# A quarter of the attention's softmax sums moved from ScalarE passes to GpSimd additions, with a shorter fill between indirect transfers and a new order

## The chip, the cores and the metric

The kernel runs on one core of one Trainium2 chip. The metric is the device time in microseconds of one execution. TensorE (PE) does the matmuls, with its weight loads listed as PEld; VectorE (DVE) and ScalarE (ACT) work on PSUM and SBUF; GpSimd (POOL) works on SBUF and issues the indirect transfers; SyncE (SP) issues the other transfers.

## What is computed

Input x has 16 batches of 512 tokens with 128 features. Three sublayers follow each other, each on the layer norm of x and added to x:

```python
x = x + 0.5 * ffn(layernorm(x))      # stage A
x = x + attention(layernorm(x))      # stage B
x = x + 0.5 * ffn(layernorm(x))      # stage C

def ffn(x):                          # 8 experts of 256 hidden units, the best 2 of each token
    probs = softmax(x @ gate_w.T + gate_b)
    vals, idx = top_k(probs, 2)
    y = relu(x @ w1[e] + b1[e]) @ w2[e] + b2[e]     # for the two experts
    return sum(y * vals)

def attention(x):                    # 8 heads of 32, 512 x 512 scores per head and batch
    q = x @ Wq.T
    k, v = (x @ Wkv_down.T) @ Wk_up.T, (x @ Wkv_down.T) @ Wv_up.T
    attn = softmax(q @ k.T * 32 ** -0.5)
    return (attn @ v) @ Wo.T
```

All data are float32.

## The kernel before

**Stages and steps.** The work is cut into named steps, keyed by stage, batch (or chunk of batches), name and number. Stages A and C route their tokens in chunks of 1 to 3 batches: gate logits, the two best experts (top1, top2, gate), the ranks of the tokens within each expert (rank1, rank2), a scatter of token rows to slots in DRAM (scat, two indirect transfers per 128 tokens on POOL), loads of four slot tiles at a time and of their experts' weights (xload, wload on SP), the expert's two products (xg, h, y), a store of the results (ystore), a gather of each token's two results (gat, two indirect transfers on POOL) and their weighted addition to x (comb, DVE). The first batch in A and the last in C are done densely instead, over all eight experts (dh, dy).

**Attention.** Each batch has two groups of four heads, and each group four tiles of 128 rows. The steps of a group are, in order:

- max or rmax: PE makes the scores with queries as rows, 4 matmuls of 128x512 per step into 4 PSUM banks; DVE takes each row's negated maximum (line 1538, neg_m). In rmax ACT then makes a second pass over the same bank (line 1199): exp(score - maximum) in place, with the row sum accumulated into `sums`; the bank is free after that. In max the bank is free after DVE.
- msplit or rsplit: rsplit takes the logarithm of the sums on ACT (line 1206) and subtracts it from neg_m on DVE (line 1545); both then split neg_m into a high and a low part. mrow: PE turns these into rows.
- s: PE makes the transposed scores and adds the rows from mrow; ACT takes the exponential into `probs` (line 1190), 4 passes of 128x512 per step, 4 steps. `probs` holds one group.
- pv: PE multiplies `probs` with V, 16 matmuls; ACT copies the result to `o_n` (line 1211).
- For a group that isn't by rows: add (line 1056), POOL adds probability tiles in pairs into `pairs`, four 128x512 additions after the second s step and four after the fourth; sum (lines 1268, 1560 and 1822): PE multiplies `pairs` with ones, 8 matmuls; ACT takes 1/sum as exp(-ln); DVE refines that and multiplies `o_n` by it. For a group by rows the probabilities are normalized already and neither step exists.
- wo: after both groups, PE multiplies `o_n` with Wo, and DVE adds it to x.

`by_rows(b, g)` at line 62 says which way a group goes; before the change it is true for all 32 groups, and no add or sum step is made. The lines that ACT's first s step waits for are at 1186: with a group before it that isn't by rows, it waits for that group's last addition (p_added). `previous_added` finds the last such group, whose `pairs` must have been read.

**The order.** A planner in the kernel's file (`all_steps`, `plan`) lays out every engine's instructions once, when the program is built. Each step has a due time, worked out from the constants at lines 90 to 100, and a cost per engine in the table PARTS (line 176; an addition on POOL stands at 1.27 us). Whenever an engine is free, the planner gives it the ready step with the earliest due time. On the chip each engine runs its list strictly in that order and waits on semaphores. Rings limit what is under way: 8 PSUM banks in all, and up to 8 for rmax, 7 for steps that DVE reads, 6 for steps that ACT reads.

**The fill.** POOL's steps scat and gat issue two indirect transfers each. Between two such steps that follow each other directly, POOL first writes the tile `pause` (line 1072, a memset of 128x900) and waits for it. The planner keeps such steps GAP (3.4 us) apart.

Of the kernel before, what the change touches and what calls it, by code (L numbers as in the profile page):

```python
# [12 lines left out]
P = 128  # L13
# [30 lines left out]
def n_quads(c):  # L44
    return (n_tiles(c) + 3) // 4
# [14 lines left out]


def by_rows(b, g):
    return True


def previous(b, g):
# [3 lines left out]
def previous_added(b, g):  # L70

    b, g = previous(b, g)
    while b >= 0 and by_rows(b, g):
        b, g = previous(b, g)
    return b, g


def max_name(b, g):
    return "rmax" if by_rows(b, g) else "max"


def split_name(b, g):
    return "rsplit" if by_rows(b, g) else "msplit"
# [3 lines left out]

PERIOD, FIRST_B = 54.81, 448.4  # L90
WANTED = {"norm": -306.42, "scaled": 175.09, "xT": -0.86, ("q", 0): -510.52, ("k", 0): -55.28, ("v", 0): 51.75,
          ("v", 1): 77.62, ("q", 1): -259.95, ("k", 1): -286.69, "wo": -16.36}
GROUP_GAP, MAX_PACE, S_FIRST, S_PACE, PV, ADD, SUM = -6.56, 9.75, -155.58, 14.86, -20.5, 31.84, 190.16
A_LEAD, A_PACE, A_ROUTE, A_NORMS = 1.91, 10.45, 102.08, 3.43
C_NORM, C_ROUTE, C_FIRST, C_PACE, C_GATHER = 70.53, 4.33, 52.37, 59.65, -48.02
LOAD_AHEAD, W_AHEAD = -185.66, -51.27
B_SHIFT = [-90.73, 208.24, -383.83, -10.9, 27.39, -56.91, -109.2, -98.67, -258.75, 51.94, -111.41, -70, -88.21, -77.68, 72.17, 64.26]
A_SHIFT = [-175.05, -104.61, -123.83, -99.41, 64.11, 103.6, 44.98]
C_SHIFT = [47.89, 123.22, 85.45, 65.66, 50.22, -503.25, 389.89]
GAP = 3.4  # L100


def wanted_attention(b):

    at = {}
    for name in ("norm", "scaled", "xT"):
        at[name, 0] = WANTED[name]
    at["wo", 0] = WANTED["wo"]
    for name, k in (("q", 0), ("k", 0), ("v", 0), ("v", 1), ("q", 1), ("k", 1)):
        at[name, k] = WANTED[name, k]  # L110
    for g in range(GROUPS):
# [8 lines left out]
        if not by_rows(b, g):  # L120
            at["sum", g] = at["pv", g] + SUM
    return {("B", b, name, k): FIRST_B + PERIOD * b + B_SHIFT[b] + t for (name, k), t in at.items()}


def wanted_experts(s, c):
# [3 lines left out]
    dense = c == DENSE[s]  # L129
    shift = (A_SHIFT if s == "A" else C_SHIFT)[c - CHUNKS_OF[s][0]]  # L130
    quads = 0 if dense else n_quads(c)
# [308 lines left out]
def plan(steps):  # L440
# [21 lines left out]
    def note(t, kind, step, part):  # L462
        nonlocal counter
        counter += 1
        put(events, (t, counter, kind, step, part))
# [5 lines left out]
    def may_begin(step):  # L471
        nonlocal next_comb
        if step.part == 0:
# [12 lines left out]
            if step.name == "comb" and combs[next_comb] != step.key[:2]:  # L486
                return False
            if step.name in ("scat", "gat") and now < indirect + GAP:
                return False
# [8 lines left out]
    while True:  # L498
        progress = True
        while progress:  # L500
            progress = False
            for e in ENGINES:
# [10 lines left out]
                if step.part == 0:  # L513
# [21 lines left out]
                    if step.name in ("scat", "gat"):  # L535
                        indirect = now
                        note(now + GAP, "look", step, 0)
                length = step.parts[step.part][1]
# [162 lines left out]
def macaron_kernel(nc, x, wq, wkv_down, wk_up, wv_up, wo, gate_w, gate_b, w1, b1, w2, b2, out):  # L701
# [41 lines left out]
    with ExitStack() as ctx:  # L743
        def sb(name, shape, dt=F32):
            return ctx.enter_context(nc.sbuf_tensor(name, shape, dt))
# [8 lines left out]
        gw_T, gate_bias = sb("gw_T", [P, EXPERTS]), sb("gate_bias", [P, EXPERTS])  # L754
        first_wins = sb("first_wins", [P, EXPERTS])
        ident = sb("ident", [P, P])
        pause = sb("pause", [P, 900])
        ones = sb("ones", [P, P])
        minus_one = sb("minus_one", [1, P])
        earlier = sb("earlier", [P, P])  # L760
# [1118 lines left out]
```

## Time and profile before

| | |
|---|---|
| median of 3 runs | 1188.9 us (1188.76 to 1192.47) |
| the profiled execution | 1187.95 us |
| its span, first to last instruction | 1186.2 us |
| mean granted TensorE clock | 0.978 of full |
| matmul records, weight-load records | 8142, 8142 |

The page of a profile gives each engine's busy time in the span, the chain of work that ended last (followed back from the last instruction, at each step to what released it), and the costliest groups of instructions. Other views answer for a stretch of time: busy time of each engine, the chain by line, or the instructions in order of time. A float32 matmul leaves two records. Matmuls are pipelined and their ends are modelled, so a busy PE isn't a PE at its peak. All matmuls outside transposes have the helper's line, 1584, so they are told apart by the tiles that they read. A row of busy time by stretch gives the stretch, its length, then PE, PEld, DVE, ACT and POOL with their instructions.

### The profile page before, as it was taken

What the parts mean: (1) busy time and instruction counts of PE and PEld (TensorE: products, weight loads), DVE (VectorE), ACT (ScalarE), POOL (GpSimd) and SP (SyncE); (2) the same over time, 40 slices, a digit from 0 to 9 for tenths busy, and PEclk for the clock granted to TensorE, in tenths of its full rate; (3) what the DMA queues carried; (4) which work ended last, traced back from release to release, by engine and by line L of the source; (5) the groups of instructions that cost most, each with busy time, mean ns of one, the idle gap of its engine ahead of it and who ended that gap; (6) DMA issues with size and microseconds to landing.
All of it is one profiled execution on the core that took longest, in us unless ns stands there. A gap on an engine that the chain in (4) does not pass through costs nothing.

```text
span 1186.2 us, 25770 instructions
## 1 busy us (share of the span) xinstructions
PE 1116.0 (94%) x8142; PEld 736.6 (62%) x8142; DVE 720.2 (61%) x2254; ACT 910.1 (77%) x2255; POOL 712.1 (60%) x868
## 2 busy tenths in 40 slices
PE   5989998999999999999999999999999999999896
PEld 3657575676675557566665666666665446657574
DVE  4766468576785557376664686556556646557335
ACT  2339678788897989797898888888888988788431
POOL 3136558674758888028888643886602885268555
PEclk9979998999999999999999999999999999999988
DMA  8074573856645177656565636576732155648872
GB/s 288 2 273 146 176 210 111 257 155 207 205 136 152 45 224 218 174 154 201 173 199 167 180 113 193 154 221 183 210 107 65 39 181 158 184 142 242 256 239 74
DMA packets 159882, 202.05 MB, mean 170 GB/s; under 512 B 16938, under 2 KB 103426, under 8 KB 159747
## 3 DMA queue, kind: packets, MB, share of 16 engines
q1 hardware_dynamic: 144196, 168.90, 46.5%
q0 software_dynamic: 15360, 31.49, 9.1%
q8 instruction: 67, 1.10, 0.4%
q14 instruction: 67, 0.55, 0.2%
q10 hardware_dynamic: 192, 0.02, 0.0%
HBM read 152.50 MB, written 47.84 MB: 169 GB/s over the span
## 4 chain that ended last, share of the span: by engine, by line
PE 70%; ACT 17%; DVE 4%; POOL 4%; issue 3%; DMA 2%; SPq 0%; POOLq 0%; ACTq 0%; DVEq 0%
PE psum L1584 65%; ACT psum L1199 7%; ACT probs L1190 6%; PE psum L1702 2%; POOL Y L1108 2%; DVE neg_m L1538 2%; PE psum L1767 1%; ACT hg L1236 1%; POOL pause L1072 1%; PE psum L1669 1%; ACT xnB L1155 1%; DMA results_C<-ys 1%; DMA xs<-slots_C 1%; DVE neg_hl L1557 0%; PE psum L1662 0%
## 5 line engine op out<-in xcount | busy, mean ns | idle before, releaser
L1538 DVE TENSOR_REDUCE neg_m<-psum 128x1 f32<-128x512 f32 x512 | 317.4, 682 | 153.1 <-PE psum L1584 152.9
L1584 PE MATMUL psum<-nat 32*128 32x512 f32 x2048 | 362.4, 637 | 0.9 <-ACT nat L1266 0.4
L1199 ACT ACTIVATE psum<-psum,neg_m 128x512 f32<-128x512 f32 x512 | 341.0, 680 | 26.5 <-DVE neg_m L1538 25.8
L1190 ACT ACTIVATE probs<-psum 128x512 f32<-128x512 f32 x512 | 266.4, 631 | 42.7 <-PE psum L1584 42.4
L1584 PEld LDWEIGHTS psum<-nat 32*128 32x128 f32 x2048 | 130.5, 184 | 93.4 <-issue 25.5
L1584 PEld LDWEIGHTS psum<-xg_T,wt 128*128 128x128 f32 x1296 | 157.4, 195 | 43.7 <-ACT probs L1190 13.6
L1072 POOL MEMSET pause<- 128x900 f32 x212 | 183.3, 865 | 0.1
L1584 PE MATMUL psum<-xg_T,wt 128*128 128x128 f32 x1296 | 172.5, 283 | 7.9 <-DMA wt<-packed 6.0
L1088 POOL DMA_INDIRECT slots_A<-xnA,posA x120 | 117.6, 980 | 91.0 <-DMA xs<-slots_A 40.9
L1584 PEld LDWEIGHTS psum<-wt,hg 128*128 128x128 f32 x1296 | 151.9, 192 | 31.6 <-ACT psum L1199 11.8
L1108 POOL DMA_INDIRECT Y<-results_C,posC x120 | 115.6, 963 | 90.2 <-issue 69.7
L1584 PE MATMUL psum<-wt,hg 128*128 128x128 f32 x1296 | 162.2, 278 | 7.9 <-ACT hg L1236 3.7
L1088 POOL DMA_INDIRECT slots_C<-xnC,posC x120 | 117.0, 975 | 56.5 <-DVE posC L1487 21.2
L1108 POOL DMA_INDIRECT Y<-results_A,posA x120 | 115.6, 963 | 57.4 <-issue 30.3
L1584 PE MATMUL psum<-m_rows,heads_one 32*128 32x512 f32 x512 | 126.9, 751 | 0.0
L1236 ACT ACTIVATE hg<-psum 128x512 f32<-128x512 f32 (+1 forms) x168 | 96.8, 621 | 35.2 <-PE psum L1584 35.1
L1584 PE MATMUL psum<-probs,V 128*32 128x512 f32 x1024 | 117.6, 600 | 5.5 <-ACT probs L1190 5.2
L1518 DVE TENSOR_TENSOR ys<-psum,wt 128x512 f32<-128x512 f32 x84 | 56.7, 675 | 99.3 <-PE psum L1584 98.9
L1199 ACT ACTIVATION_READ_ACCUMULATOR psum<-psum,neg_m 128x1 f32 x512 | 115.8, 226 | 0.0
L1123 POOL TENSOR_SCALAR xnC<-X,rstdC,shiftC 128x128 f32<-128x128 f32 x64 | 28.5, 454 | 119.1 <-DVE shiftC L1370 118.8
L1584 PEld LDWEIGHTS psum<-probs,V 128*32 128x32 f32 x1024 | 31.6, 110 | 73.3 <-issue 59.8
L1211 ACT ACTIVATE o_n<-psum 128x512 f32<-128x512 f32 x32 | 19.1, 596 | 54.1 <-PE psum L1584 53.8
(190 smaller groups left out, 1382.2 us busy)
## 6 DMA issues: line engine op xcount, KB each, us to landing
wt<-packed SPq DMA_DIRECT2D x324, 320.0 KB
xs<-slots_A SPq DMA_DIRECT2D x36, 256.0 KB
results_A<-ys SPq DMA_DIRECT2D x36, 256.0 KB
xs<-slots_C SPq DMA_DIRECT2D x36, 256.0 KB
results_C<-ys SPq DMA_DIRECT2D x36, 256.0 KB
X<-in_L_attn_x_dram SPq DMA_DIRECT2D x16, 256.0 KB, 7.9
out_dram<-X SPq DMA_DIRECT2D x16, 256.0 KB
packed<-probs SPq DMA_DIRECT2D x1, 2560.0 KB, 8.2
```

What stands on the lines that cost most here:

```text
L1072: linked(pool.memset(pause[:], 0.0))
L1088: pool.indirect_dma_start(out=slots[s][:], out_offset=bass.IndirectOffsetOnAxis(ap=pos[s, c % C_RING][:, k, t:t + 1], axis=0), in_=xn[s][: ...
L1108: pool.indirect_dma_start(out=Y[:, i % Y_RING, k, n, :], out_offset=None, in_=results[s, c][:], in_offset=bass.IndirectOffsetOnAxis(ap=pos ...
L1123: last = pool.tensor_scalar(xn[s][:, xn_place(s, b) + n, :], X[:, b % X_RING, n, :], rstd[s][:, n:n + 1], shift[s][:, n:n + 1], ALU.mult, ...
L1190: act.activation(probs[:, kt, j, :], at.banks()[j][:], ACT.Exp).then_inc(a_done, 1)
L1199: act.activation(at.banks()[j][:], at.banks()[j][:], ACT.Exp, bias=neg_m[:, g, n, j:j + 1], accum_out=sums[:, g, n, j:j + 1]).then_inc(S[" ...
L1211: act.activation(o_n[:, at.k, :], bank[:], ACT.Copy).then_inc(a_done, 1)
L1236: act.activation(hg[:, i % HG_RING, 0:n, :, :].rearrange("p n u t -> p (n u t)"), bank[:, 0:n * UNITS * P], ACT.Relu).then_inc(a_done, 1)
L1518: V_.tensor_tensor(ys[:, i % YS_RING, 0:len(tiles), :], bank[:, 0:len(tiles) * P].rearrange("p (i d) -> p i d", d=D), wt[:, first:first + ...
L1538: V_.tensor_reduce(neg_m[:, g, n, j:j + 1], at.banks()[j][:], AX.X, ALU.max, negate=True).then_inc(S["r_done"], 1)
L1584: return nc.tensor.matmul(dst, w, m, start=start, stop=stop)
L1702: last = nc.tensor.transpose(bank[:, tokens(n)], xs[:, i % XS_RING, n, :], ident[:])
```

## The change

`by_rows` becomes true for group 1 of every batch and group 0 of the even batches: group 0 of the 8 odd batches, a quarter of the groups, now takes max, msplit, add and sum instead of rmax and rsplit. The tile `pause` shrinks from 900 to 400 columns, and the planner's GAP from 3.4 to 2.95 us. All due-time constants are new, so the order of every engine is laid out anew. Costs in PARTS, rings and buffers stay.

```diff
 def by_rows(b, g):
-    return True
+    return g == 1 or b % 2 == 0
...
-PERIOD, FIRST_B = 54.81, 448.4
-WANTED = {"norm": -306.42, "scaled": 175.09, "xT": -0.86, ("q", 0): -510.52, ("k", 0): -55.28, ("v", 0): 51.75,
-          ("v", 1): 77.62, ("q", 1): -259.95, ("k", 1): -286.69, "wo": -16.36}
-GROUP_GAP, MAX_PACE, S_FIRST, S_PACE, PV, ADD, SUM = -6.56, 9.75, -155.58, 14.86, -20.5, 31.84, 190.16
+PERIOD, FIRST_B = 55.55, 516.37
+WANTED = {"norm": -221.79, "scaled": 160.9, "xT": 66.34, ("q", 0): -644.14, ("k", 0): -62.88, ("v", 0): 53.33,
+          ("v", 1): 27.43, ("q", 1): -402.5, ("k", 1): -375.9, "wo": 48.96}
+GROUP_GAP, MAX_PACE, S_FIRST, S_PACE, PV, ADD, SUM = -42.62, 6.88, -135.18, 13.63, -2.2, 24.62, 228.05
...
-GAP = 3.4
+GAP = 2.95
...
-        pause = sb("pause", [P, 900])
+        pause = sb("pause", [P, 400])
```

The lines left out between SUM and GAP are the other due-time constants (A_LEAD to C_SHIFT), all with new values.

## Rows read from the trace of the kernel before

**Rows 1.** The page's head: busy us, share of the span, instructions of each engine.

```profile
span 1186.2 us, 25770 instructions
...
PE 1116.0 (94%) x8142; PEld 736.6 (62%) x8142; DVE 720.2 (61%) x2254; ACT 910.1 (77%) x2255; POOL 712.1 (60%) x868
```

**Rows 2.** The chain that ended last: by engine (page), by line (whole chain).

```profile
PE 70%; ACT 17%; DVE 4%; POOL 4%; issue 3%; DMA 2%; SPq 0%; POOLq 0%; ACTq 0%; DVEq 0%
...
by line: PE psum L1584 64.9%; ACT psum L1199 6.8%; ACT probs L1190 6.4%; issue 3.3%; PE psum L1702 2.3%; POOL Y L1108 1.8%; DVE neg_m L1538 1.5%; PE psum L1767 1.2%; ACT hg L1236 0.9%; POOL pause L1072 0.8%; PE psum L1669 0.8%; ACT xnB L115
```

**Rows 3.** Busy us by stretch and engine; clock, DMA share, GB/s.

```profile
918.00:962.00 44.00, 41.04 (x233) 20.83 (x229) 25.16 (x55) 41.48 (x107) 36.40 (x42) 1.00 0.17 52
200.00:1100.00 900.00, 874.09 (x6598) 562.98 (x6590) 558.11 (x1645) 764.90 (x1907) 564.23 (x646) 1.00 0.56 168
```

**Rows 4.** Chain by line: 200 to 1100, 918 to 962, 420 to 441.

```profile
by line: PE psum L1584 71.1%; ACT psum L1199 8.4%; ACT probs L1190 7.2%; PE psum L1702 2.6%; issue 1.9%; PE psum L1767 1.5%; ACT xnB L1155 0.9%; ACT hg L1236 0.8%; DVE neg_m L1538 0.8%; DMA xs<-slots_C 0.7%; PE psum L1669 0.7%; PE psum L166
...
by line: ACT psum L1199 41.8%; ACT probs L1190 31.3%; PE psum L1584 13.4%; DVE neg_hl L1557 3.0%; issue 2.3%; DVE neg_m L1538 1.6%; PE psum L1767 1.5%; ACT m_rows L1215 1.4%; ACT nat L1266 1.1%; ACT V L1175 1.1%; ACT log_sums L1206 0.7%; AC
...
by line: PE psum L1584 64.4%; DMA xs<-slots_C 30.3%; PE psum L1702 6.2%; issue 0.6%
```

**Rows 5.** Instruction groups: count, busy us, mean ns, idle us before and releasers.

```profile
L1199 ACT ACTIVATE psum<-psum,neg_m 128x512 f32<-128x512 f32 x512 | 341.0, 680 | 26.5 <-DVE neg_m L1538 25.8
...
L1190 ACT ACTIVATE probs<-psum 128x512 f32<-128x512 f32 x512 | 266.4, 631 | 42.7 <-PE psum L1584 42.4
...
L1523 DVE TENSOR_TENSOR X<-psum,X 128x512 f32<-128x512 f32 x16 | 10.9, 684 | 8.9 <-PE psum L1584 8.9
...
L1206 ACT ACTIVATE log_sums<-sums 128x16 f32<-128x16 f32 x32 | 8.0, 250 | 0.4
```

**Rows 6.** Timeline 920 to 938 us: start, us, engine, line, idle before.

```profile
922.59 0.66 ACT L1199 ACTIVATE psum<-psum,neg_m 128x512 f32<-128x512 f32 x1
...
923.26 0.65 ACT L1199 ACTIVATE psum<-psum,neg_m 128x512 f32<-128x512 f32 x1
...
924.59 0.66 ACT L1199 ACTIVATE psum<-psum,neg_m 128x512 f32<-128x512 f32 x1
...
924.75 0.29 PEld L1584 LDWEIGHTS psum<-nat 32*128 32x128 f32 x2 [0.38 <-ACT psum L1199]
```

**Rows 7.** Timeline from 470 us: batch 5, last s pass, pv, next group.

```profile
473.65 2.08 ACT L1190 ACTIVATE probs<-psum 128x512 f32<-128x512 f32 x4
...
475.82 3.64 PE L1584 MATMUL psum<-probs,V 128*32 128x512 f32 x32 [0.26 <-ACT probs L1190]
...
479.39 1.14 PE L1584 MATMUL psum<-nat 32*128 32x512 f32 x8
...
480.79 2.06 ACT L1190 ACTIVATE probs<-psum 128x512 f32<-128x512 f32 x4 [0.67 <-PE psum L1584]
```

**Rows 8.** POOL's instruction groups, columns as in rows 5.

```profile
L1072 POOL MEMSET pause<- 128x900 f32 x212 | 183.3, 865 | 0.1
...
L1123 POOL TENSOR_SCALAR xnA<-X,rstdA,shiftA 128x128 f32<-128x128 f32 x64 | 27.7, 442 | 48.6 <-DVE shiftA L1370 46.6 <-DMA slots_A<-xnA,posA 1.7
...
L1034 POOL MEMSET ones<- 128x128 f32 x1 | 0.2, 201 | 0.0
```

**Rows 9.** The end: chain by line from 1108 us, timeline from 1170.

```profile
by line: POOL Y L1108 26.8%; issue 17.9%; POOL pause L1072 12.1%; DMA results_C<-ys 11.8%; PE psum L1584 7.1%; ACT probs L1190 3.7%; DMA Y<-results_C,posC 3.1%; DVE X L1503 2.6%; SPq L996 2.2%; SPq L997 2.1%; POOLq L743 1.5%; DVE X L1462 1.
...
1172.03 3.73 PE L1584 MATMUL psum<-probs 128*128 128x128 f32 x32
...
1174.17 0.86 POOL L1072 MEMSET pause<- 128x900 f32 x1
...
1176.57 0.95 POOL L1108 DMA_INDIRECT Y<-results_C,posC  x1 [0.30 <-issue]
1179.04 2.31 DVE L1503 SCALAR_TENSOR_TENSOR X<-Y,gateC,X 128x128 f32<-128x128 f32 x8 [3.17 <-DMA Y<-results_C,posC]
...
1181.99 1.13 DVE L1462 SCALAR_TENSOR_TENSOR X<-psum,givenC,X 128x128 f32<-128x128 f32 x4
```

More of the change, by code:

```diff
@@ L83, in split_name @@
     return "rsplit" if by_rows(b, g) else "msplit"
-PERIOD, FIRST_B = 54.81, 448.4
-WANTED = {"norm": -306.42, "scaled": 175.09, "xT": -0.86, ("q", 0): -510.52, ("k", 0): -55.28, ("v", 0): 51.75,
-          ("v", 1): 77.62, ("q", 1): -259.95, ("k", 1): -286.69, "wo": -16.36}
-GROUP_GAP, MAX_PACE, S_FIRST, S_PACE, PV, ADD, SUM = -6.56, 9.75, -155.58, 14.86, -20.5, 31.84, 190.16
[L94 to L99, printed above, removed]
-GAP = 3.4
+PERIOD, FIRST_B = 55.55, 516.37
+WANTED = {"norm": -221.79, "scaled": 160.9, "xT": 66.34, ("q", 0): -644.14, ("k", 0): -62.88, ("v", 0): 53.33,
+          ("v", 1): 27.43, ("q", 1): -402.5, ("k", 1): -375.9, "wo": 48.96}
+GROUP_GAP, MAX_PACE, S_FIRST, S_PACE, PV, ADD, SUM = -42.62, 6.88, -135.18, 13.63, -2.2, 24.62, 228.05
+A_LEAD, A_PACE, A_ROUTE, A_NORMS = 20.81, 7.22, 126.74, 5.62
+C_NORM, C_ROUTE, C_FIRST, C_PACE, C_GATHER = 45.48, 46.92, 69.4, 56.84, -148.48
+LOAD_AHEAD, W_AHEAD = -228.24, -52.47
+B_SHIFT = [-112.91, 194.63, -374.71, -81.81, 45.44, -91.1, -114.34, -112.13, -293.69, 43.01, -104.38, 4.57, -63.69, -89.57, 34.33, 66.2]
+A_SHIFT = [-283.55, -71.81, -31.91, -95.18, 13.23, 110.89, 85.61]
+C_SHIFT = [22.45, 143.53, 208.16, 83.05, -88.11, -661.1, 395.16]
+GAP = 2.95
 def wanted_attention(b):
```

## The prediction

> **What bounds the kernel now.** I read the page's head first: TensorE (PE) is busy for 94% of the span, ScalarE (ACT) for 77%, VectorE (DVE) 61% and GpSimd (POOL) 60% [rows 1]. A PE that is busy for 94% looks like the bound, so the second view is the chain of work that ended last, and it says something more careful: 70% of the span hangs on PE, but 17% on ACT, and of that 6.8% of the span (0.068 x 1186.2 = 81 us) on line 1199 and 6.4% (76 us) on line 1190 [rows 2]. Line 1199 is the second pass over the score rows that makes the softmax sums (step rmax); line 1190 makes the probabilities (step s).
>
> The third view is busy time by stretch. From 200 to 1100 us, PE is busy for 874 of 900 us and ACT for 765. From 918 to 962 us PE still shows 41.0 of 44 us, yet ACT is at 41.5 there [rows 3], and the chain of that stretch is ACT: 41.8% on line 1199 and 31.3% on line 1190, against 13.4% on PE's line 1584 [rows 4]. So a busy PE in that stretch is a PE that crawls: its matmuls are spread out by the wait for a free PSUM bank. The timeline shows it: ACT starts a pass every 0.67 us (922.59, 923.26, ..., 924.59) and PE's weight loads wait 0.38 us on line 1199 for the bank that such a pass gives back [rows 6]. In other stretches the same step costs nothing: from 420 to 441 us, where batch 5's group 0 makes its maxima and sums, line 1199 isn't on the chain at all [rows 4]. The kernel is thus bound by PE for most of the time and by ACT in patches of the attention.
>
> The end is a third regime. After the last attention step the chain runs through POOL's gathers, and 12.1% of the last 79 us, 9.6 us, is the fill (pause) between them, that is 11 of them [rows 9].
>
> **The change part by part.**
>
> **ACT is relieved.** Group 0 of each odd batch, 8 of 32 groups, goes from rmax/rsplit to max/msplit. That takes 8 x 16 = 128 passes of line 1199 away, at a spacing of 0.67 us: -86 us of ACT time [rows 5, 6], and 8 logarithms of 0.25 us: -2 us [rows 5]. Each sum step gives ACT a logarithm and an exponential of 128x512 back, at about 0.63 us as line 1190's: 8 x 2 x 0.63 = +10 us [rows 5]. Net -78 us of 910. Only what is on the chain counts. A quarter of line 1199's 81 us is -20 us. From one side this could be 0, if the chain's patches lie in the other groups, as between 420 and 441 us. From the other it could be about -39 us, if the s passes that queue behind the removed ones leave the chain in the same proportion ((81 + 76) / 4). I take -20: it is the mean over all groups. The 10 us of added ACT work count by ACT's 17% of the chain: +2 us.
>
> **PE gets eight sum steps.** Each is 8 matmuls of ones with 32 output rows, four of which share a round as those of pv do: pv's 16 take 479.39 - 475.82 = 3.57 us [rows 7], so 8 take 1.79 us and the eight steps 14.3 us. Nothing on PE goes away: the maxima's matmuls stay. At PE's 70% of the chain this is +10 us; the ends are 0, if all of it falls into ACT's patches, and +14.3 us.
>
> **DVE.** Its maxima stay. The three operations per sum step, near 0.68 us each as line 1523's [rows 5], add 8 x 3 x 0.68 = 16 us to an engine at 61%, while group 1 is still being worked; wo needs them only after group 1's pv. Nothing on the path, 0. If the cover failed (wo waiting for the sum), the whole step would show, 1.8 on PE, 2 x 0.63 on ACT and 3 x 0.68 on DVE, about 5 us in each odd batch. Where msplit replaces rsplit the wait for ACT's logarithm falls out, on the path perhaps -1 us.
>
> **POOL gets 64 additions of 128x512**, which the trace doesn't show. From below: a memset of 128 columns takes 0.20 us and one of 900 takes 0.865 us, 0.86 ns a column, so 512 columns that are only written take 0.53 us. From above: a tensor_scalar of 128 columns takes 0.44 us and four of them 1.77 us [rows 8], or 3.5 us if a second input costs as much again. An addition reads SBUF as the tensor_scalar does, in one instruction instead of four, so I take a value near its first figure, 1.4 us; the kernel's own cost table counts 1.27. 64 x 1.4 = 90 us, and the shorter fill gives 212 x 0.43 = 92 us back (below), so POOL's load stays. The Trainium skill speaks against this move: "GPSIMD Engine Reference", section 4.1 Engine selection, sends additions of a tile to VectorE, since a two-input operation is about twice as slow on GpSimd. No row here shows such an operation on GpSimd; with line 1523's 684 ns the rule would make an addition an estimated 1.4 us and leave the sum as it is. At the tensor_scalar's 3.5 us the sum would be 12 us higher (below).
>
> **A new wait.** ACT's first probability pass of the next group waits for the last addition, because the additions read the single buffer of probabilities. Queued behind it on ACT are all later passes, and PE waits for the banks they empty. Four additions come after a group's last s pass: 4 x 1.4 = 5.6 us. Today the next group's first pass starts 480.79 - 475.73 = 5.1 us after the end of that last pass (473.65 + 2.08), behind pv [rows 7]. The additions are then 0.5 us late by themselves; POOL works in order, and half a spacing of the indirect transfers under way (1.5 us) comes on top: about 2 us in each of 8 groups, 16 us of ACT time, of which 17% reaches the end: +3 us. Ends: 0 at 0.53 us an addition; at 3.5 us they are 9 + 1.5 us late, 84 us of ACT time and +14 us, some 12 above what I take; and +16 us if PE has no expert work to put into the 2 us.
>
> **The fill.** By the two memset rows 400 columns take 0.20 + 272 x 0.00086 = 0.43 us instead of 0.865: -0.43 us a pause. At the end 11 of them are on the chain: -4.8 us. There PE finishes its last matmuls at 1175.8 us and POOL issues its last gather at 1176.57; the combination on DVE starts at 1179.04 and the last expert's additions, which stood behind it, end at 1183.1 [rows 9]. PE's end is just behind POOL's, so the dense expert is late next: of the 4.8 us I count -4; ends 0 and -5. At the start, the first scatter and gather have about three pauses each, -2 us if they are on the path; I count -1.
>
> **The replanned order.** The due times change everywhere. The trace gives no price for that; I count 0. From the stretch of 200 to 1100 us, where 26 of 900 us are idle on PE [rows 3], an order better or worse by about half of that is plausible: -12 to +12 us.
>
> **The sum:** -20 + 2 + 10 - 1 + 3 - 4 - 1 = -11 us. The profiled execution took 1187.95 us with a span of 1186.2; the median of the runs is 1188.9, 0.95 us above it. 1187.95 - 11 = 1177, and about 1178 for a median.
>
> **The rivals.**
>
> *PE pays in full (slower).* Place: PE's stretches where its line 1584 makes up the chain, 71.1% from 200 to 1100 us [rows 4]. If ACT's patches lie in groups that keep their row sums, the relief is near 0, while the sums cost 14.3 us, the late additions 3 and the fill gives 5 back: 1189 + 12 = 1201 us. It decides once less than 8 us of the relief reaches the chain. For it: the stretch at 420 us. Against it: that of 920 us, in which batch 13's group 0 has its passes, with line 1199 on 41.8% of the chain [rows 4].
>
> *Late additions (slower).* If additions stand behind two spacings of indirect transfers (2 x 2.95 us, the plan's new gap) and cost 1.77 us each, ACT restarts 13 us after the last pass instead of 5: up to 8 x 8 = 64 us of ACT time; a third of it at the end gives about 1189 - 11 + 21 = 1199 us, more if PE runs dry. Against it: POOL is idle for 40% of the span [rows 1].
>
> *The whole patch goes (faster).* Relief of -39 instead of -20: 1159 us, with a better order down to 1150.
>
> *No difference.* Relief and sums cancel, and only the fill is left, or an order that is worse by some 8 us: 1186 to 1192 us.
>
> *The fill isn't what spaces the transfers*, so shortening it does nothing: the pauses on the chain, each between two gathers [rows 9], speak against it; it would cost the 5 us of gain, 1183 us.
>
> **How the numbers follow.** Forecast (1164 to 1185, the fill's rival in it): 0.45. Whole patch: 0.11. No difference, within 0.3% (3.6 us, about what a measurement of this kernel can tell): 0.14. PE in full: 0.20. Late additions: 0.10. So faster 0.56, same 0.14, slower 0.30. The forecast's own range is 1164 to 1185. The range for 8 in 10 takes in most of both slower rivals and of the whole patch: 1152 to 1206.
>
> **What would show it.** Right: line 1199 with 384 passes and about 85 us less busy; ACT's share of the chain near 15.5% (202 - 18 of 1175 us), PE's near 71.5% (830 + 10); 128 records of ones with pairs, two per matmul, eight matmuls spaced 1.8 us in all; pauses of 0.43 us and a tail shorter by 4 us; additions of 1.2 to 1.6 us, with ACT's wait on them under 2 us. Wrong: ACT's share of the chain still at 17% with PE's work 14 us longer; waits of line 1190 on POOL's additions of 5 us and more; a later end of the dense expert in the tail; idle PE in the middle beyond today's 26 us, which would put the loss on the new order.

## The result, and the profile after

The changed kernel takes 1208.8 us (median of four runs, 1203.9 to 1215.0) against 1189.2 us (median of four): 1.0146 times the time before, with a 95% interval of 1.0115 to 1.0176. The ratios here and below are those on record, from runs side by side; they aren't the quotients of the medians (here 1.016). A second measurement of the same code gave 1207.9 us and 1.0151 [1.0096, 1.0206]. The forecast was 1178 us in a range of 1152 to 1206; the sign is wrong and the time lies outside the range.

The profiled execution took 1215.0 us with a span of 1212.9, and is the slowest of the four. From its page come the span, the busy times, the granted TensorE clock in 40 slices, and the groups of the moved step (busy us, mean ns, idle us before and what ended it):

```profile
span 1212.9 us, 25879 instructions
...
PE 1142.3 (94%) x8270; PEld 748.9 (62%) x8270; DVE 747.0 (62%) x2270; ACT 837.6 (69%) x2007; POOL 697.8 (58%) x917
...
PEclk9978998999999898999889999999999989999989
...
L1199 ACT ACTIVATE psum<-psum,neg_m 128x512 f32<-128x512 f32 x384 | 255.8, 680 | 25.0 <-DVE neg_m L1538 24.2
...
L1064 POOL TENSOR_TENSOR pairs<-probs 128x512 f32<-128x512 f32 x64 | 79.9, 1280 | 34.6 <-ACT probs L1190 34.5
L1072 POOL MEMSET pause<- 128x400 f32 x197 | 88.5, 449 | 0.1
...
L1827 PE MATMUL psum<-pairs,ones 128*32 128x512 f32 x128 | 15.4, 598 | 0.7 <-ACT psum L1199 0.7
```

Nearly all of what the change says has happened. Line 1199 has 384 passes instead of 512 and is busy for 85.2 us less [rows 5], an addition takes 1.28 us, a pause 0.45 us, the eight sum steps 15.4 us on PE, and ACT is down from 910.1 to 837.6 us, by 72.5 [rows 1]. Two lines don't fit a kernel that lost work. DVE rose by 26.8 us [rows 1], where 16 us of sums were expected. And the clock row, nothing but nines from the eighth slice to the 38th before, has five slices with an 8 there, while PE stays at 94% busy.

The stretch from 200 to 1100 us shows why the busy share misled (stretch, length, then PE, PEld, DVE, ACT and POOL with their instructions, granted clock, DMA share, GB/s):

```profile
200.00:1100.00 900.00, 879.09 (x6554) 565.25 (x6554) 570.14 (x1632) 696.04 (x1684) 528.48 (x655) 0.97 0.54 161
```

PE is idle for 20.9 us here, less than the 25.9 us before [rows 3]. But it left 6554 matmul records instead of 6598, although the whole kernel has 128 more, and its granted clock is 0.97 instead of 1.00. Against the kernel before, the time didn't go into idle PE; PE runs slower here. The order differs, though, and with it the work that falls into the stretch. The kernel new_writes (below) has the changed kernel's own order, and against it both show, 7.2 us more of idle PE and a lower clock. Its row:

```profile
200.00:1100.00 900.00, 886.27 (x6739) 569.86 (x6740) 562.91 (x1671) 707.90 (x1717) 530.29 (x671) 0.99 0.55 166
```

To find the places I compared when each batch's output addition starts (line 1523, the sixteen times in order) with the same times of a kernel that differs only in what POOL does in place of the additions (new_writes, below). The changed kernel falls behind in jumps: +3.4 us in batch 1, +5.4 in batch 5, +7.1 in batch 7, +4.4 in batch 13 and +3.3 in batch 15, and by no more than 0.5 us in any other batch. All are odd batches, the ones with additions. These two profiles stand at opposite ends, the slowest of four runs against the fastest of ten (1190.5 us), so the jumps add up to more than the 15 us between the kernels' runs. A second profile of the changed kernel (changed_again, 1207.9 us, at its median) starts 2.2 us ahead of new_writes and is 17.1 us behind at batch 15, with +3.8 us in batch 1, +3.9 in batch 5, +1.7 in batch 7, +2.6 in batch 9, +4.2 in batch 13 and +3.3 in batch 15: odd batches again.

Batch 5's jump, in order of time (start, us, engine, line, idle before and what ended it):

```profile
466.50 0.16 DVE L1361 SCALAR_TENSOR_TENSOR ntC<-ntC,vepsC 128x4 f32<-128x4 f32 x1
...
467.58 4.94 POOL L1064 TENSOR_TENSOR pairs<-probs 128x512 f32<-128x512 f32 x4 [2.05 <-ACT probs L1190]
...
467.85 1.01 DVE L1360 TENSOR_TENSOR ntB<-rstdB 128x4 f32<-128x4 f32 x1 [0.60 <-ACT rstdB L1147]
...
468.90 1.20 DVE L1361 SCALAR_TENSOR_TENSOR ntB<-ntB,vepsB 128x4 f32<-128x4 f32 x1
...
470.13 1.19 DVE L1362 SCALAR_TENSOR_TENSOR rstdB<-ntB,rstdB 128x4 f32<-128x4 f32 x1
...
471.35 1.19 DVE L1369 TENSOR_TENSOR shiftB<-mvB,rstdB 128x4 f32<-128x4 f32 x1
...
472.65 2.48 DVE L1538 TENSOR_REDUCE neg_m<-psum 128x1 f32<-128x512 f32 x4
...
472.78 1.65 ACT L1155 ACTIVATE xnB<-X,shiftB,rstdB 128x128 f32<-128x128 f32 x4 [3.50 <-DVE shiftB L1370]
...
475.14 1.36 PE L1584 MATMUL psum<-nat 32*128 32x512 f32 x3 [2.80 <-ACT psum L1199]
```

Four additions run on POOL from 467.58 to 472.52. Beside them DVE works through four operations on 128x4 elements, the normalisation's Newton step and shift. Each has two inputs in SBUF and takes 0.16 us where POOL adds nothing (so at 466.50, a microsecond earlier); here each takes as long as an addition. The chain is done at 472.7 instead of some 469. ACT waits 3.50 us for it, the maxima on DVE (line 1538) stand behind it, and PE runs dry for 2.80 us.

The other jumps have the same form. Between 195 and 1125 us PE is idle for more than 1.3 us at a time in five places: 1.81 us before 239 us (batch 1), 2.80 before 475 (batch 5), 1.36 before 599 (batch 7), 2.35 before 981 (batch 13) and 1.66 before 1113 (batch 15). In the ten us ahead of each, DVE instructions are held beside additions. In new_writes no idle time of PE in that stretch is longer than 1.14 us. Batch 13's is the plainest, with the low part of the negated maxima (line 1558) held and PE waiting for it:

```profile
977.50 4.95 POOL L1064 TENSOR_TENSOR pairs<-probs 128x512 f32<-128x512 f32 x4 [6.46 <-ACT probs L1190]
...
980.07 1.20 DVE L1558 TENSOR_TENSOR neg_hl<-neg_m,neg_hl 128x16 f32<-128x16 f32 x1
...
981.41 0.76 PE L1767 MATMUL psum<-ident,neg_hl 128*128 128x128 f32 x4 [2.35 <-DVE neg_hl L1558]
```

After a stall the clock can follow. Three stretches of ten us around batch 5's, columns as above, for the changed kernel:

```profile
455.00:465.00 10.00, 9.57 (x74) 6.43 (x71) 9.29 (x33) 9.97 (x27) 7.97 (x11) 1.00 0.60 183
465.00:475.00 10.00, 7.34 (x60) 5.11 (x52) 9.05 (x22) 6.47 (x18) 7.46 (x8) 1.00 0.64 181
475.00:485.00 10.00, 9.86 (x46) 6.08 (x47) 5.05 (x24) 8.47 (x23) 4.66 (x7) 0.66 0.76 227
```

In the last one PE is busy for 9.86 us with only 46 matmuls, at a mean granted clock of 0.66: by the trace's clock records it stood at the lower level, 1.2 GHz, from 476.6 to 483.4 us. So the stall of some 3 us is paid a second time in slow matmuls. The two profiles of the changed kernel give a price for that. In changed_again the same stall (2.81 us) is followed by 3.4 us at the lower level instead of 6.8, and the jump is 3.9 us instead of 5.4; in batch 7 the same stall (1.35 us) is followed by none instead of 13.7 us in two patches, and the jump is 1.7 us instead of 7.1. By these two pairs a microsecond at the lower level cost about 0.4 us (an estimate: 1.5 us over 3.4, and 5.4 over 13.7). Over the whole span the records show 94.6 us at the lower level in 12 patches; before it was 52.4 us in 7.

Counted over the trace, 26 DVE instructions beside an addition last over 0.15 us longer than the median of their group, together 31.7 us: lines 1360, 1361, 1362 and 1369 of the normalisation, 1441, 1443, 1476, 1478 and 1484 of the routing, 1545, 1557 and 1558 of msplit and rsplit, and 1503. Before, a different pair did this: 41 DVE instructions beside a pause of 900 columns, 27.3 us in all.

The Trainium skill has this rule on its page "SBUF — State Buffer", section "Who interferes with whom": a DVE instruction with two SBUF inputs contends with a GpSimd instruction that reads SBUF, though not with one that only writes it, and copies, casts and tensor_scalars in their two-port mode contend with any; the loser waits for the whole instruction. The trace agrees in kind, with 1.01 to 1.20 us beside additions of 1.28 us on average. It is the rule that spoke against this change, and the prediction didn't weigh it.

### The profile page after: what moved, and what is told of

It reads as the page before. It is cut to its first block and busy times, and to the rows that moved or that the text cites. A ratio compares the mean times of both kernels' runs of the same rounds, so it can differ in the third digit from the quotient of the medians.

```text
span 1212.9 us, 25879 instructions
## 1 busy us (share of the span) xinstructions
PE 1142.3 (94%) x8270; PEld 748.9 (62%) x8270; DVE 747.0 (62%) x2270; ACT 837.6 (69%) x2007; POOL 697.8 (58%) x917
## 5 line engine op out<-in xcount | busy, mean ns | idle before, releaser
L1199 ACT ACTIVATE psum<-psum,neg_m 128x512 f32<-128x512 f32 x384 | 255.8, 680 | 25.0 <-DVE neg_m L1538 24.2
L1584 PEld LDWEIGHTS psum<-xg_T,wt 128*128 128x128 f32 x1296 | 165.2, 201 | 46.6 <-ACT probs L1190 14.8
L1584 PE MATMUL psum<-xg_T,wt 128*128 128x128 f32 x1296 | 182.0, 290 | 3.5 <-DMA wt<-packed 3.0
L1108 POOL DMA_INDIRECT Y<-results_A,posA x120 | 115.3, 961 | 72.5 <-issue 37.1
L1584 PE MATMUL psum<-m_rows,heads_one 32*128 32x512 f32 x512 | 130.3, 787 | 0.0
L1518 DVE TENSOR_TENSOR ys<-psum,wt 128x512 f32<-128x512 f32 x84 | 56.0, 668 | 72.3 <-PE psum L1584 63.6
L1064 POOL TENSOR_TENSOR pairs<-probs 128x512 f32<-128x512 f32 x64 | 79.9, 1280 | 34.6 <-ACT probs L1190 34.5
L1072 POOL MEMSET pause<- 128x400 f32 x197 | 88.5, 449 | 0.1
L1199 ACT ACTIVATION_READ_ACCUMULATOR psum<-psum,neg_m 128x1 f32 x384 | 86.5, 225 | 0.0
```

What stands on the lines that cost most here:

```text
L1064: pool.tensor_tensor(pairs[:, kt // 2, j, :], probs[:, kt - 1, j, :], probs[:, kt, j, :], ALU.add).then_inc(S["p_added"], 1)
L1072: linked(pool.memset(pause[:], 0.0))
L1108: pool.indirect_dma_start(out=Y[:, i % Y_RING, k, n, :], out_offset=None, in_=results[s, c][:], in_offset=bass.IndirectOffsetOnAxis(ap=pos ...
L1199: act.activation(at.banks()[j][:], at.banks()[j][:], ACT.Exp, bias=neg_m[:, g, n, j:j + 1], accum_out=sums[:, g, n, j:j + 1]).then_inc(S[" ...
L1518: V_.tensor_tensor(ys[:, i % YS_RING, 0:len(tiles), :], bank[:, 0:len(tiles) * P].rearrange("p (i d) -> p i d", d=D), wt[:, first:first + ...
L1584: return nc.tensor.matmul(dst, w, m, start=start, stop=stop)
```

## The experiments

Those that rest on the kernel before are named old_..., those on the changed kernel new_.... An inserted line moves the line numbers behind it by one to three.

**The cause: what the additions do to others.** new_writes puts a memset of 1020 columns in each addition's place and lets it wait for the one before, so POOL is busy nearly as long but reads nothing; the ones' product reads a constant.

```diff
-                pool.tensor_tensor(pairs[:, kt // 2, j, :], probs[:, kt - 1, j, :], probs[:, kt, j, :],
-                                   ALU.add).then_inc(S["p_added"], 1)
+                if (at.index, at.k) == (1, GROUP):
+                    pool.memset(pairs[:], 1.0)
+                wait(pool, S["p_added"], counts["p_added", at.step] - 1)
+                pool.memset(written[:], 0.0).then_inc(S["p_added"], 1)
```

> The changed kernel, order unchanged; each addition is replaced by a memset of 1020 columns and a wait for the one before it, about the time of an addition, which reads no SBUF (the sums are then constants). In the changed kernel's trace 26 VectorE instructions, most with two SBUF inputs, are stretched by 31.7 us in all beside additions. If that blocking is what stalls TensorE and lowers its clock: 1193 to 1203 us, with these instructions at their usual length. If only the additions' time and place count: 1206 to 1212 us.

It took 1194.7 us, 1.0019 [0.9998, 1.0041] times the time before: by the two ratios 1.3% less than the changed kernel, 15 us. The same place in its timeline, and the same stretches:

```profile
464.00 4.15 POOL L1068 MEMSET written<- 128x1020 f32 x4 [1.74 <-ACT probs L1193]
...
464.30 0.16 DVE L1363 TENSOR_TENSOR ntB<-rstdB 128x4 f32<-128x4 f32 x1 [0.61 <-ACT rstdB L1150]
...
464.89 0.16 DVE L1372 TENSOR_TENSOR shiftB<-mvB,rstdB 128x4 f32<-128x4 f32 x1
465.09 0.95 DVE L1373 TENSOR_SCALAR shiftB<-shiftB 128x4 f32<-128x4 f32 x1
...
466.07 1.65 ACT L1158 ACTIVATE xnB<-X,shiftB,rstdB 128x128 f32<-128x128 f32 x4 [0.35 <-DVE shiftB L1373]
...
465.00:475.00 10.00, 9.91 (x70) 6.49 (x67) 7.83 (x29) 9.62 (x26) 8.45 (x11) 1.00 0.94 276
475.00:485.00 10.00, 10.00 (x87) 5.30 (x89) 1.40 (x3) 5.34 (x12) 7.87 (x9) 1.00 0.46 138
```

Beside writes the four operations take 0.16 us again; the tensor_scalar behind them (line 1373 here) is the one that is held up, for 0.95 us. ACT waits 0.35 us instead of 3.50, PE doesn't stall, and the clock stays at 1.00. DVE's busy time falls from 747.0 to 720.7 us and the time at the lower clock from 94.6 to 52.7 us. The memsets aren't free for DVE either: 17 instructions are held beside them, by 14.3 us in all, but PE doesn't stall for it. The memset's series is shorter than the additions' (4.15 against 4.94 us), so a little of the 15 us could be POOL's time; the next kernel bounds that.

new_addtiny replaces each addition by a memset of a single column: no reads, and hardly any time on POOL.

```diff
-                pool.tensor_tensor(pairs[:, kt // 2, j, :], probs[:, kt - 1, j, :], probs[:, kt, j, :],
-                                   ALU.add).then_inc(S["p_added"], 1)
+                if (at.index, at.k) == (1, GROUP):
+                    pool.memset(pairs[:], 1.0)
+                n = counts["p_added", at.step] - 1
+                pool.memset(ticks[:, n:n + 1], 0.0).then_inc(S["p_added"], 1)
```

> The changed kernel, order unchanged; each addition is replaced by a memset of one column, about 0.1 us (the sums are then constants): POOL's 80 us, the blocking of VectorE and nearly all of ScalarE's wait for the last addition are gone, the sum steps stay. If additions cost the changed kernel its loss: 1185 to 1197 us. If the loss lies in the order and in TensorE's sums: 1203 to 1209 us.

1192.4 us, 0.9991 [0.9972, 1.0009]: only 0.28%, 3.3 us, below new_writes, with intervals that overlap, though POOL is busy for another 58.2 us less. POOL's time and the holding that memsets do are worth some 3 us; what hurts is the reading. Its time at the lower clock is 68.4 us, more than new_writes' 52.7, and it is still no slower: the microseconds at the lower level aren't a measure of the loss by themselves.

**Shorter blocks?** If a blocked operation waits for one POOL instruction, four pieces of 128 columns would cut the wait to a quarter. changed_again is the changed kernel itself beside it.

```diff
-                pool.tensor_tensor(pairs[:, kt // 2, j, :], probs[:, kt - 1, j, :], probs[:, kt, j, :],
-                                   ALU.add).then_inc(S["p_added"], 1)
+                for n in range(4):
+                    part = slice(n * P, (n + 1) * P)
+                    last = pool.tensor_tensor(pairs[:, kt // 2, j, part], probs[:, kt - 1, j, part], probs[:, kt, j, part], ALU.add)
+                last.then_inc(S["p_added"], 1)
```

> The changed kernel, order unchanged; each addition of 512 columns is made in four instructions of 128. POOL's time for them goes up by its fixed part, some 0.1 us an instruction, 20 us in all. Theory blocking for the length of one GpSimd instruction: each stretched VectorE instruction loses about 0.4 us instead of up to 1.2, so some 20 of 32 us go; ratio 1.002 to 1.010 in spite of longer additions. If VectorE has to wait until GpSimd has no reading instruction left, or if the additions' length counts instead: 1.014 to 1.025.

> The changed kernel as it is, beside the others of this set on the same chip. If its loss holds against the kernel before: ratio 1.010 to 1.018, with TensorE at half clock for 80 to 105 us and VectorE instructions stretched by about 30 us beside additions.

new_chop4 took 1216.7 us, 1.0215 [1.0187, 1.0242], the changed kernel beside it 1207.9, 1.0151 [1.0096, 1.0206]: no better. Its group of additions, then a stretch of its timeline:

```profile
L1066 POOL TENSOR_TENSOR pairs<-probs 128x128 f32<-128x128 f32 x256 | 109.2, 463 | 18.7 <-ACT probs L1192 18.5
...
860.78 6.63 POOL L1066 TENSOR_TENSOR pairs<-probs 128x128 f32<-128x128 f32 x16
...
862.53 4.50 DVE L1547 TENSOR_TENSOR neg_m<-neg_m,log_sums 128x16 f32<-128x16 f32 x1 [2.08 <-ACT log_sums L1208]
...
867.82 0.45 PE L1769 MATMUL psum<-ident,neg_hl 128*128 128x128 f32 x1 [3.15 <-DVE neg_hl L1560]
```

Four pieces cost 1.85 us instead of 1.28. In many places the hold did shrink with the pieces: three of batch 5's four operations take 0.38 or 0.39 us each instead of 1.19 or 1.20, and batches 5 and 7 fall behind new_writes by 2.1 and 1.2 us. But one operation of 128x16 elements, 0.19 us by itself [before's group has a mean of 194 ns], was held for 4.50 us, over some eleven pieces of 0.41 us, to within 0.4 us of the end of the series; batch 11, where it stands, falls behind by 6.0 us. Three other operations beside the pieces take 4.3 to 5.6 us each. So the theory that an operation is blocked for one POOL instruction falls as a rule. The changed kernel has such a case too: the operation on line 1441 starts while POOL issues a gather and ends with the four additions that follow.

```profile
1106.52 5.58 DVE L1441 TENSOR_SCALAR gateC<-rs 128x4 f32<-128x4 f32 x1
...
1107.12 4.94 POOL L1064 TENSOR_TENSOR pairs<-probs 128x512 f32<-128x512 f32 x4
```

The page of the Trainium skill named above lets the loser wait for one instruction; these two rows show more, and the measurement decides. Why one operation gets in after one instruction and another only after the whole series, no run here settles.

**Does reading hurt by itself?** old_fillreads is the kernel before with a pause that reads: an addition over 330 columns.

```diff
-        pause = sb("pause", [P, 900])
+        pause = sb("pause", [P, 3, 110])
...
-                    linked(pool.memset(pause[:], 0.0))
+                    read = ones[:, 0:110].unsqueeze(1).to_broadcast([P, 3, 110])
+                    linked(pool.tensor_tensor(pause[:], read, read, ALU.add))
```

> The kernel before, order unchanged; the fill between indirect transfers is an addition of 3 x 110 columns that reads SBUF instead of a memset of 900, about as long (0.8 to 0.95 us). If a reading GpSimd instruction blocks VectorE's instructions with two SBUF inputs: those (lines 1360 to 1369, 1503, 1545) are stretched where they meet a fill, 20 to 40 us in all, and the time is 1195 to 1210 us against 1189 to 1194 of before. If reading plays no part: within 3 us of before.

1194.0 us, 1.0011 [0.9990, 1.0032]: within the 3 us that had been put down to reading playing no part. Its pauses and combinations:

```profile
L1073 POOL TENSOR_TENSOR pause<-ones 128x330 f32<-128x330 f32 x212 | 160.4, 757 | 4.8
...
L1504 DVE SCALAR_TENSOR_TENSOR X<-Y,gateC,X 128x128 f32<-128x128 f32 x120 | 43.1, 419 | 4.7 <-DMA Y<-results_C,posC 4.2
...
L1504 DVE SCALAR_TENSOR_TENSOR X<-Y,gateA,X 128x128 f32<-128x128 f32 x120 | 42.5, 415 | 19.1 <-DMA Y<-results_A,posA 18.6
```

The combination's operations, two inputs in SBUF, are longer: 415 and 419 ns, where before they took 349 and 347. So reading does hold DVE, and the time hardly moves. DVE instructions are stretched by 42 us in all by the count above, but in the kernel before it was 27 us already, so 15 us are added. The pauses are also 0.11 us shorter, worth some 2 us by old_fill400 (an estimate from its 8.8 us for 0.42 us), so a cost of a few us can be hidden here; the 15 us of the changed kernel can't. The difference that the traces show: here single operations are held up, by a microsecond at most, while in the changed kernel's batch 5 four instructions in a row stand on the chain from statistics to maxima and lose 4 us together. That the place on the chain decides is argued from this; no run varies it alone.

**The fill.** old_fill400 and old_fill128 shorten the pause in the kernel before, with its order kept; new_fill900 gives the changed kernel the old pause.

```diff
-        pause = sb("pause", [P, 900])
+        pause = sb("pause", [P, 400])
```

> The kernel before with the fill of 400 columns alone; order and row sums unchanged. Theory fill-helps: 4 to 5 us less in the tail (11 pauses on the chain, 0.43 us each) and VectorE's casts and small tensor_scalars, which in the trace of before are stretched by about 27 us in all in 41 places that overlap a pause memset, come out shorter: 1178 to 1185 us. Theory fill-harms (denser indirect transfers cost more than they give): 1195 us or more. Theory fill-idle: 1189 us.

> The kernel before, order unchanged, with a fill of 128 columns (0.20 us instead of 0.865 us). The fill of 400 gave a ratio of 0.9926. If the gain is the tail's pauses and the VectorE casts that met a long fill: 0.987 to 0.992, a little more than with 400. If transfers that follow each other so closely get into each other's way: 1.00 or more.

> The changed kernel with the fill of 900 columns put back, order unchanged. If the short fill is what made the changed kernel slower: 1195 us or less. If the short fill helps as predicted: 1213 to 1225 us, with POOL later and more VectorE work stretched by pauses. If it plays no part: 1209 us.

old_fill400: 1183.8 us, 0.9926 [0.9898, 0.9955]; old_fill128: 1185.1 us, 0.9937 [0.9916, 0.9958]. Both beat both kernels; below 400 columns nothing more comes. From old_fill400's page, and the cast of line 1557 (in the kernel before, x32, its mean is 478 ns):

```profile
span 1178.4 us, 25770 instructions
...
PE 1119.4 (95%) x8142; PEld 740.4 (63%) x8142; DVE 703.4 (60%) x2254; ACT 909.4 (77%) x2255; POOL 624.5 (53%) x868
...
L1557 DVE CAST neg_hl<-neg_m 128x16 fp32r<-128x16 f32 x32 | 8.8, 276 | 1.1
```

Batch 15's output addition starts at 1117.1 us instead of 1119.7, and the rest takes 61.3 us instead of 66.5: 2.6 us ahead of the tail and 5.2 in it. Neither part is firm. With the pause of 900 the same stretch takes 64.4 us in old_relief's profile and 63.6 in old_pv6's, so the tail's gain is 2 to 5 us; and of the 2.6 us ahead, 2.1 lie before batch 0's output addition (146.6 against 148.7 us). A shorter write holds DVE's casts up less, and DVE is 16.8 us less busy [rows 1]; that this reached the end isn't shown.

new_fill900: 1257.5 us, 1.0576 [1.0507, 1.0645], 4.2% above the changed kernel, some 50 us for 82 us more of pauses. With GAP at 2.95 the order counts on the short pause. This is what the short pause is worth to this order, not what it brings to the other. Its tail, from batch 15's output addition on, takes 70.7 us against the changed kernel's 66.4.

**Relief and price, each alone.** old_relief is the kernel before, in which the 128 passes of line 1199 in group 0 of the odd batches are copies of one column. old_pv6 has eight more matmuls in pv of those groups, the number a sum step has.

```diff
+                    if at.index % 2 and g == 0:
+                        act.activation(sums[:, g, n, j:j + 1], ones[:, 0:1], ACT.Copy).then_inc(S["r_summed"], 1)
+                        continue
```

```diff
-                for kt in range(TILES):
+                rounds = [0, 1, 2, 3, 0, 1] if at.index % 2 and g == 0 else [0, 1, 2, 3]
+                for i, kt in enumerate(rounds):
```

> The kernel before, order unchanged; in group 0 of the odd batches ScalarE's 128 second passes over the scores are left out (a copy of one column stands in their place, so these groups' probabilities aren't normalized). It is the relief of the change alone: 0.67 us a pass less about 0.2 us of the stand-in, some 60 us of ScalarE time. Theory of the prediction (a quarter of line 1199's 81 us on the chain): 1170 to 1176 us. Rival, that the order and TensorE set the time and the relief is swallowed: 1186 to 1190 us. If the banks that come back earlier let TensorE run on: below 1168 us.

> The kernel before, order unchanged; in group 0 of the odd batches pv makes six rounds of four matmuls instead of four (two of them a second time, so the output isn't the reference's): 8 x 1.79 = 14.3 us more on TensorE, the work of the sum steps without their other parts. Prediction: +10 us, between 0 and +14.3. If TensorE's stalls swallow it: 1189 to 1192 us. If TensorE is the bound throughout: 1203 us or more.

old_relief: 1184.4 us, 0.9918 [0.9887, 0.9949], 9.8 us less. Its page:

```profile
PE 1114.0 (94%) x8142; PEld 740.3 (63%) x8142; DVE 720.1 (61%) x2254; ACT 848.8 (72%) x2127; POOL 712.4 (60%) x868
...
L1202 ACT ACTIVATE psum<-psum,neg_m 128x512 f32<-128x512 f32 x384 | 256.3, 683 | 21.0 <-DVE neg_m L1541 20.8
```

ACT is 61.3 us less busy here, since the copies stay; scaled to the 78 us of the step that is an estimated -12.5 us. old_pv6: 1206.1 us, 1.0112 [1.0075, 1.0149], 13.3 us more for 64 matmuls, near the 14.3 us of the full price.

**Move and order.** new_allrows takes the changed kernel's constants and fill, with the sums of all groups in the rows again. old_move keeps the old constants and fill and moves the quarter.

```diff
 def by_rows(b, g):
-    return g == 1 or b % 2 == 0
+    return True
```

> The changed kernel's constants and fill, but all 32 groups by rows: no additions, no sum steps; the planner lays the order out for that. If the move of the sums costs the 20 us (14.8 us of TensorE work, additions that hold up VectorE, stalls that lower TensorE's clock): 1180 to 1192 us. If the new order costs it: 1203 to 1215 us.

> The kernel before with a quarter of the groups moved to additions and sums, constants and fill of before; the planner lays the order out for that. If the move costs the 20 us whatever the order: 1203 to 1220 us. If the new order costs it: 1180 to 1195 us.

1233.9 us, 1.0352 [1.0313, 1.0391], and 1239.6 us, 1.0385 [1.0348, 1.0422]: both are worse than either kernel, and outside what either theory had expected. A set of due times fits the mix that it was made for, and so neither run gives the price of the order or of the move by itself. These two are inconclusive.

## Why the prediction was wrong, step by step

**What bounds the kernel.** The reading held. PE for most of the time and ACT in patches is what old_pv6 (nearly the full price) and old_relief (a part of 61 us) show.

**ACT is relieved: -20 us, and +2 for the sums' own work on ACT.** Right in kind, too large: an estimated -12.5 us for both in the kernel before (-17 to -8 by the interval of old_relief). The quarter of line 1199's share of the chain took all groups alike; the two stretches read for it had already shown one group on the chain and one off it [rows 4].

**PE gets eight sum steps: +10 us.** Too small: +13.3 us in old_pv6 (8.9 to 17.7), close to the end of 14.3. PE's 70% of the chain was used as a chance that an added matmul counts. Since relief and price come out as -12.5 and +13.3, the trade of ACT's passes for PE's matmuls brings nothing that these runs can tell from zero, even without any contention.

**DVE: nothing on the path, 0.** This is the step that failed. The cover for the three added operations was weighed, and the effect of POOL's reads on the DVE instructions that were already there wasn't. It is worth some 15 us (the changed kernel against new_writes), and it reaches the end through the chain from the normalisation to the maxima (batch 5), through the split of the maxima (batch 13) and through the routing (batch 15), with the granted clock behind it. It is about half of the miss. From the forecast of -11 us to the measured +18 there are some 29 us; new_addtiny, the whole change without its additions, stands at -1 us (-3 to +1), where the prediction's other terms add up to -14. So without the reads the change would have been no faster than before, and the rest of the miss lies in the other terms.

**POOL's additions, 1.4 us each, and the new wait, +3 us.** The duration was 1.28 us. The wait isn't there: in the changed kernel's trace the next group's first probability pass starts 1.8 to 22.8 us after the last addition, and none of ACT's idle time is put down to POOL. That new_writes and new_addtiny differ by 3.3 us is no confirmation of the term, since ACT doesn't wait for the additions. The additions were priced as POOL's time and ACT's wait alone, and that made the range too narrow as well: neither the ends of this term nor a rival held the contention.

**The fill: -5 us, none of it through DVE.** In the kernel before it is -8.8 us, 2 to 5 of them in the tail. In the changed order the tail is no shorter: from batch 15's output addition to the end it takes 66.4 us, as before. The chains of these ends by line, changed kernel from 1146 to 1213 us, then old_fill400 from 1115 to 1190 us, of which its span fills 63 us:

```profile
by line: POOL Y L1108 31.5%; DMA results_C<-ys 26.8%; issue 11.4%; POOL pause L1072 7.5%; DVE X L1503 6.0%; DMA Y<-results_C,posC 3.6%; POOLq L743 1.8%; SPq L996 1.3%; DVE X L1462 1.3%; SPq L997 1.2%; DVE ys L1518 1.0%; DVE psum L1459 0.9%;
```

```profile
by line: PE psum L1584 55.4%; DMA wt<-packed 10.2%; DVE X L1462 2.7%; DVE X L1503 2.6%; issue 1.8%; SPq L996 1.8%; DVE psum L1459 1.8%; PE psum L1702 1.6%; SPq L997 1.2%; DVE ys L1518 0.9%; PE psum L1669 0.8%; DVEq L743 0.3%; SPq L994 0.1%
```

In old_fill400 the pauses are off the chain and PE's dense expert is late next, as forecast. In the changed order the gathers wait for the stores of the last results (results_C, 26.8% of 67 us instead of 11.8% of 79 us [rows 9]), and more of them are left: 34 gathers with 16 pauses stand behind batch 15's output addition, where before it was 24 with 11. The shorter pause helps there too, as the 70.7 us of new_fill900 show, and the new order takes the gain back.

**The order: 0, ±12.** Not measured by itself. Put together from the runs, in us: -12.5 (relief) + 13.3 (PE) - 8.8 (fill) + 15 (reads) + 3.3 (POOL's time) = +10.3, against some 18 measured. The tail that is no shorter is 2 to 5 us of the difference, by the traces alone; the rest is within the intervals of the terms, which come from different orders. The range of 12 us for a new order was no bound: new_allrows and old_move came out 42 and 46 us above the kernel before, though with constants made for another mix. How much of the 15 us is the clock's isn't settled: the 0.4 us a microsecond come from two places, and new_addtiny is no slower with more time at the lower level.

**The rivals.** "PE pays in full" named the right size for PE, but it took the relief as near 0, which old_relief contradicts, and ended at 1201 us; "late additions" found the right instruction and the wrong victim. In batch 5 the additions end at 472.5, and it is DVE that waits for them, not ACT.

**What would show it.** The signs that concern the moved work came true: passes, additions, pauses, the sum's matmuls. The shorter tail didn't, and ACT's share of the chain can't be compared, since the changed kernel's chain can be followed back only to 1033 us. The sign of a loss in the middle, more idle PE than before, didn't show: PE idled less, at a lower clock, and only against new_writes, with the same order, did it idle more. A granted clock that falls should have been on the list.

## What to carry to other kernels

Before work goes to GpSimd, list what it reads and writes in SBUF, and look which of DVE's small instructions run beside it in a chain that somebody waits for: their price is the length of the GpSimd instruction, or of its whole series, not their own. Compare matmuls per stretch and the granted clock, not PE's busy time, and do so against a kernel of the same order where there is one, since a PE that was stalled may be busier and slower afterwards. And try the cheap part of a change alone: here the shorter fill, without anything else, was the gain.

## What the runs showed of the hardware

- A DVE operation of 128x4 elements with two SBUF inputs takes 0.16 us alone or beside a GpSimd memset, and 1.0 to 1.2 us beside a GpSimd addition of 1.28 us. A tensor_scalar or a cast is held up by a memset as well: 0.95 us beside one of 1020 columns, and the cast of line 1557 takes 478 ns on average with pauses of 900 columns and 276 with 400.
- One operation can be held beyond one GpSimd instruction: 5.58 us over a gather's issue and four additions, 4.50 us over eleven short pieces.
- A GpSimd addition takes 1280 ns for 128x512 and 463 ns for 128x128: a quarter of the columns costs 36% of the time.
- After a PE stall of 2.80 us at full clock, the granted clock was at the lower level for 6.8 us; after the same stall in a second profile of the same kernel (2.81 us), for 3.4 us.
